# Three edits in a mixture-of-experts, scan and soft-expert kernel: gates spread by DMA, a first sequence started another way, eight logit tiles computed a stage earlier

## What is computed

```python
# 1. mixture of experts: a shared expert of 512 units, 8 routed experts of 128 units, top 2 of 8
s = sigmoid(x_flat @ router_w.T + t_bias)
combine = gates of the two largest s, zero for the other six        # [tokens, 8]
H = gelu(einsum('nd,ehd->enh', x_flat, rw1))
O = einsum('enh,edh->end', H, rw2)
cond = (shared_out + einsum('end,ne->nd', O, combine)) / 3
# 2. two selective scans (forward and on the flipped sequence), 512 channels x 16 states, 1024 steps
h = exp(delta * A) * h + (delta * u) * B ;  y_t = sum over states of h * C
# 3. gated mix of both directions, projection, residual, then a mask by a threshold per column
x1 = x + proj(g * y_f + (1 - g) * y_b) ;  xm = x1 where |x1| >= threshold
# 4. soft experts: 64 experts x 32 slots
logits = einsum('bmd,dnp->bmnp', xm, phi)
dispatch = softmax(logits, axis=0)            # over the two batches
combine = softmax(logits over all n*p)        # per token
out = x1 + combine-weighted sum of (slots @ W + b)
```

## Time and profile before

| what | value |
|---|---|
| median of 3 runs | 1508.34 us (1508.3 to 1510.53) |
| the profiled execution | 1510.97 us, of which 1509.2 us from the first to the last instruction |
| PE busy | 1202.4 us (80%) |
| DVE busy | 1144.5 us (76%) |
| POOL busy | 888.9 us (59%) |
| ACT busy | 776.6 us (51%) |
| mean granted PE clock | 0.889 of full |

### The profile page before, as it was taken

How to read it: one execution, slowest core, us unless ns; L and a number is a source line. 1 busy time by engine, 2 the same in 40 slices (tenths; PEclk the granted TensorE clock), 3 DMA queues, 4 the chain that set the end, 5 groups by cost and what they waited for, 6 DMA issues and landing times. The chain is left out here.

```text
span 1509.2 us, 14727 instructions
## 1 busy us (share of the span) xinstructions
PE 1202.4 (80%) x4972; PEld 670.6 (44%) x4972; DVE 1144.5 (76%) x1020; ACT 776.6 (51%) x1038; POOL 888.9 (59%) x395
## 2 busy tenths in 40 slices
PE   5899987698748897649887475473687999999998
PEld 4688842233203232113322121131246788787887
DVE  4433355999999999999999999999876544554544
ACT  5343456567546676545775555465255534343430
POOL 4420024999999999999999999999811000000000
PEclk9999999798868898769889788696798999999999
DMA  5133017322363342354223427312105030302012
GB/s 197 43 126 112 28 37 254 154 83 112 129 235 125 128 167 96 131 223 181 81 87 143 154 110 286 140 68 100 49 9 195 0 140 1 140 0 118 7 39 73
DMA packets 42544, 169.82 MB, mean 113 GB/s; under 512 B 5601, under 2 KB 10209, under 8 KB 30066
## 3 DMA queue, kind: packets, MB, share of 16 engines
q1 hardware_dynamic: 42482, 169.05, 30.2%
HBM read 136.53 MB, written 32.51 MB: 112 GB/s over the span
## 5 line engine op out<-in xcount | busy, mean ns | idle before, releaser
L1205 POOL TENSOR_TENSOR scan_dbu<-scan_rep,scan_bc 128x1024 f32<-128x1024 f32 x254 | 592.3, 2358 | 38.7 <-ACT scan_rep L1102 32.5
L1286 DVE TENSOR_TENSOR_SCAN scan_hs<-scan_hs,scan_dbu 128x1024 f32<-128x1024 f32 x189 | 432.2, 2287 | 15.7 <-ACT scan_hs L1131 14.1
L1131 ACT ACTIVATE scan_hs<-scan_rep,scan_neg_a 128x1024 f32<-128x1024 f32 x252 | 280.8, 1118 | 303.2 <-DVE scan_hc L1298 276.4
L1019 PE MATMUL scan_ysum<-scan_hc,scan_sel 128*32 128x512 f32 x1008 | 169.6, 804 | 208.5 <-DVE scan_hc L1298 193.1
L1298 DVE TENSOR_TENSOR scan_hc<-scan_hs,scan_bc 128x1024 f32<-128x1024 f32 x189 | 231.1, 1223 | 6.0
L1019 PEld LDWEIGHTS scan_ysum<-scan_hc,scan_sel 128*32 128x32 f32 x1008 | 35.3, 130 | 323.2 <-issue 269.5
L1211 POOL TENSOR_TENSOR scan_hc<-scan_hc,scan_bc 128x1024 f32<-128x1024 f32 x67 | 157.7, 2353 | 10.2 <-DVE scan_hc L1286 9.8
L1286 DVE TENSOR_TENSOR_SCAN scan_hc<-scan_hs,scan_dbu 128x1024 f32<-128x1024 f32 x67 | 152.7, 2279 | 2.0 <-POOL scan_dbu L1205 1.0
L899 PE MATMUL late_banks<-late_xin,scan_inwf 128*128 128x512 f32 x256 | 114.5, 601 | 0.0
L32 PE MATMUL ffn_sl<-ffn_tanh_s,xm_s 128*128 128x512 f32 x384 | 106.0, 411 | 2.3 <-DVE ffn_tanh_s L2031 2.3
L32 PE MATMUL moe_first<-moe_x_s,moe_w_s 128*128 128x512 f32 x384 | 98.3, 399 | 8.2 <-DVE moe_w_s L412 8.2
(11 more groups left out here) (234 smaller groups left out, 1732.0 us busy)
## 6 DMA issues: line engine op xcount, KB each, us to landing
scan_rep<-dd_rows SPq DMA_DIRECT2D x60, 1024.0 KB, 5.8
scan_bc<-bc_rows SPq DMA_DIRECT2D x32, 512.0 KB, 6.1
ffn_wt<-in_ew SPq DMA_DIRECT2D x16, 1024.0 KB, 7.3
dd_rows<-scan_dd SPq DMA_DIRECT2D x15, 1024.0 KB, 3.8
scan_inwf<-fold SPq DMA_DIRECT2D x12, 512.0 KB, 3.9
cond<-scan_bc SPq DMA_DIRECT2D x16, 256.0 KB, 3.1
y_all<-scan_yo SPq DMA_DIRECT2D x6, 512.0 KB, 3.1
scan_bc<-in_xT SPq DMA_DIRECT2D x4, 512.0 KB, 7.7
```

The source lines that it names most:

```text
L1019: mm = nc.tensor.matmul(ysum[i * D32:(i + 1) * D32, h, :], sel[:], hc[:, (s0 + i) % HCR, h * CT:(h + 1) * CT], start=False, stop=last, til ...
L1131: nc.scalar.activation(hs[:, s % HSR, :], rep[:, e % REPS, 0, :], ACT.Exp, scale=scale).then_inc(da_done, 1)
L1205: nc.gpsimd.tensor_tensor(dbu[:, s % DBR, :], rep[:, e % REPS, 1, :], bc[:, j, 0, :], ALU.mult).then_inc(dbu_done, 1)
L1286: nc.vector.tensor_tensor_scan(states, hs[:, s % HSR, :], dbu[:, s % DBR, :], 0.0, ALU.mult, ALU.add).then_inc(scan_done, 1)
```

## The change

Three edits that share a tile called `wide` (16 KB a partition). In the expert stage it holds the raw weights, in the scan stage the convolution's output of odd sequences (`uc[1]`), and from the mixing stage on the logits of one batch, and then the output sums.

1. Expert gates. In chunks 1 to 3 the expert units have no `factor`: the turned gates are copied to SBUF, stored to `gate_rows` in HBM, and SP loads each row to 128 partitions (`load_gates`, 8 DMAs of 256 KB a chunk). DVE's product reads this tile.
2. First sequence. The exponential of `neg_a` comes later on ACT. A memset goes from DVE to POOL. The first step's Relu on ACT and addition on DVE become two DVE operations that read PE's banks. PE writes the spread step straight into the decay slots (`spread_step`), the order of the spread is written out (`FIRST_SPREADS`), and DVE takes the first spread product from PSUM. Periods 0 and 1 have 3 pool units (0, 6, 11) where they had 4.
3. Last stage. PE makes the 8 logit tiles of batch 0, chunk 0, in the mixing stage ahead of every second one of the first 16 turns, and ACT copies them out. Chunk 0 of the last stage makes only batch 1's. The maximum over both is then two operations. Batch 1's `x1` rows are copied to tiles of their own (the old `gate` tile), with no wait for stores. The zeroing of the output sums goes behind chunk 0's exponentials.

```diff
+        def spread_gate(g):
+            return g >= UNITS and g % UNITS >= SU
...
+            def load_gates(c):
+                sp.wait_ge(hid_done, UNITS * c if c > 1 else 1)
+                for e in range(EXPERTS):
+                    sp.dma_start(wide_gate[:, e, :], gate_rows[c * E32 + e].partition_broadcast(P)).then_inc(gate_in[e // SU], 16)
...
+            sp.wait_ge(comb_ready, 2)
+            sp.dma_start(gate_rows, logit_sb[:]).then_inc(gate_in[0], 16)
+            sp.wait_ge(gate_in[0], 16)
+            sp.wait_ge(logits_done, 1)
+            load_gates(1)
             for c in range(NC):
                 b, h = divmod(c, CB)
+                if 0 < c < NC - 1:
+                    load_gates(c + 1)
...
             for g in range(SU + 3, NC * UNITS):
                 value(g)
-                factor(g)
+                if not spread_gate(g):
+                    factor(g)
                 project(g - 2)
...
+                if spread_gate(g):
+                    dve.wait_ge(gate_in[u // SU - 1], 16 * (SU * c + int(u < 2 * SU)))
+                    other = wide_gate[:, u - SU, :]
+                else:
+                    dve.wait_ge(factor_done, FACTORS[g])
+                    other = first[:, g % 3, 1, :]
                 dve.wait_ge(act_done, g + 1)
-                nc.vector.tensor_tensor(first[:, g % 3, 1, :], act_h[:, g % 2, :], first[:, g % 3, 1, :], ALU.mult
-                                        ).then_inc(hid_done, 1)
+                nc.vector.tensor_tensor(first[:, g % 3, 1, :], act_h[:, g % 2, :], other, ALU.mult).then_inc(hid_done, 1)
...
             nc.vector.tensor_copy(gates_s[:, 0, :], turned).then_inc(gates_ready, 1)
+            nc.vector.tensor_copy(logit_sb[:], turned).then_inc(comb_ready, 1)
...
-POOL_UNITS, LATE_POOL_UNITS = (0, 3, 7, 10, 13), (0, 4, 8, 12)
+FIRST_POOL_UNITS, POOL_UNITS, LATE_POOL_UNITS = (0, 6, 11), (0, 3, 7, 10, 13), (0, 4, 8, 12)
...
+FIRST_SPREADS = ((0, 0), (1, 0), (0, 1), (1, 1), (1, 2), (0, 2), (1, 3), (0, 3))
...
+            def spread_step(i):
+                if i >= HSR:
+                    wait_states(pe, i - HSR)
+                wait_delta(pe, 0)
+                for h in range(HALVES):
+                    mm = nc.tensor.matmul(hs[:, i % HSR, h * CT:(h + 1) * CT], spread[:, i * P:(i + 1) * P],
+                                          dd[:, 0, h * CT:(h + 1) * CT], start=True, stop=True)
+                mm.then_inc(spread_done, 1)
...
             def replica(i):
                 for h in range(HALVES):
-                    x, free = ready(act, "r", i, 1, h)
+                    x, free = ready(act, "r", i, h)
+                    if i == 0:
+                        act.wait_ge(dbu_done, 1)
...
-            nc.scalar.activation(neg_a[:], neg_a[:], ACT.Exp).then_inc(neg_done, 1)
             nc.scalar.preload_act_table_set("silu_and_others")
...
+            nc.scalar.activation(neg_a[:], neg_a[:], ACT.Exp).then_inc(neg_done, 1)
             act.wait_ge(neg_done, 2)
+            for kind, i in FIRST_SPREADS:
+                (decay, replica)[kind](i)
...
-            step_add(nc.vector, dve, 0)
+            dve.wait_ge(soft, HALVES + 2)
+            for h in range(HALVES):
+                x, free = ready(dve, "t", 0, 0, h)
+                own = dd[:, 0, h * CT:(h + 1) * CT]
+                nc.vector.scalar_tensor_tensor(own, x, 0.0, own, ALU.max, ALU.add).then_inc(free, 1)
             step_du(nc.vector, dve, 0)
...
+            def logits(m):
+                if m == 0:
+                    pe.wait_ge(kept["phi_split"], 1)
+                    pe.wait_ge(xt_low, KC)
+                    pe.wait_ge(gate_done, KC)
+                wait(pe, logits_read, m - 1)
+                for k in range(KC):
+                    mm = split_products(nc, pg[:, m % 2, :], [x[:, k, 0, m * P:(m + 1) * P] for x in xt_s],
+                                        [w[:, k, :] for w in kept["phi_s"]], k == 0, k == KC - 1)
+                mm.then_inc(logits_mm, 1)
...
-            for key in TURNS:
+            for g, key in enumerate(TURNS):
+                if g < 2 * MT and g % 2 == 0:
+                    logits(g // 2)
                 turn(*key)
...
-                        act.wait_ge(x1_stored[j % 2], 16 * TG // 2)
-                    nc.scalar.activation(turn_sb[j], tr[:, g % 2, :], ACT.Copy).then_inc(turn_read[g % 2], 1)
+                        act.wait_ge(y_done, KC * CB)
+                    nc.scalar.activation(turn_sb[b][j], tr[:, g % 2, :], ACT.Copy).then_inc(turn_read[g % 2], 1)
...
-                for b in range(BATCH):
+                for b in range(int(first), BATCH):
                     for k in range(KC):
                         mm = split_products(nc, lg[:, b, :], [x[:, k, b, m * P:(m + 1) * P] for x in xt_s],
...
-            nc.gpsimd.memset(acc[:], 0.0).then_inc(init_done, 1)
+            pool.wait_ge(exp_done, BATCH * MT)
+            pool.wait_ge(diff_done, MT)
+            nc.gpsimd.memset(acc, 0.0).then_inc(init_done, 1)
```

237 lines of the change are left out of this document (136 added, 101 removed).

## The result

The changed kernel takes 1500.31 us (median of 8 runs, 1495.5 to 1504.0), the kernel before beside it 1509.6 (8 runs, 1508.3 to 1513.5): ratio 0.9939, 95% interval 0.9924 to 0.9954, 9.3 us or 0.6% faster. Forecast were 1490.0 and a range up to 1498.5: the sign is right and half of the gain is missing. Profiled execution: 1501.33 us, span 1499.5 (before 1510.97 and 1509.2).

The account below looks back on a forecast made before the run. PE was taken to bound the expert and last stages, DVE to set the scan stage's pace beside a full POOL. Expert -8.4, scan front -4.0, mixing +1.5, last -7.4 sum to -18.3: median 1490.0 us, range 1484.5 to 1498.5.

Parts of the forecast that it names:

- term of +1.5 for the held product: Expert stage, chunk 1: DVE's product, both inputs in SBUF, held by POOL's four folding operations; +1.5 us (0 to +6).
- Rival (B): Expert stage: POOL holds DVE's product at each of four folding operations, margin under 0.53; +5 us, 1495, chance 0.10.
- term of +0.65: Expert stage: the new copy of the gates on DVE stands between two operations PE waits for; +0.65 us.
- step (a) to (c): Scan front: earlier first copy -0.7, Relus off ACT -0.5, shorter spread -2.3; first scan 3.5 us earlier.
- step (c): Scan front, spread written into decay slots: product with u to first scan takes 3.9 us, not 6.1; -2.3.
- what I had named as an end and not taken: Scan front: PE at half clock for the first spread records as before, about +1.5 us; left out of the sum.
- (d): Scan periods 0 and 1, 3 pool units: DVE's extra product of 1.2 us each is hidden; uncovered, +1.2 each.
- from then on DVE sets the pace, and a start that is earlier by some time ends earlier by the same: Scan stage: POOL holds DVE up just once, for 0.25 us, so the front's gain of 4.0 us lasts.
- rival (C): Scan stage: PE's sum for unit 11 comes 1.1 us later, DVE waits; +3.5 us, 1493.5, chance 0.11.
- +1.5 and -7.4: Mixing stage 1.5 us longer for the logits moved into it; last stage 7.4 us shorter without them.
- (A): Mixing stage: PE's clock falls between the turns; +11 us, 18 at worst, 1501, chance 0.12.
- (E): Mixing-stage logits displace nothing, first chunk held elsewhere: last stage gains 2 us, not 7.4; 1495.5, chance 0.09.

Follow-up runs that it names:

- filler of two: Changed kernel with pool units 0, 4, 8, 12 in the first two periods, plus two useless PE products ahead of the first skip product: 1489.75 us, 0.9842.
- new front with the old units: Changed kernel, but POOL weighs units 0, 4, 8, 12 in the first two periods: 1494.12, 1492.46 and 1494.95 us in three groups.
- filler of six: Changed kernel plus six useless PE products ahead of the first skip product, pool units unchanged: 1498.1 us, ratio 0.9904.
- old front: Changed kernel with its second edit undone (scan front and pool units as in the kernel before): 1496.28 us, 0.9897; one later run 1491.48.

## Why the prediction was wrong, point by point

**Expert stage: the gates' worth right, the two small terms not.** Between the marks the edit brings 11.0. The forecast had 10.6 (its 0.45 us a unit would give 10.4). The term of +1.5 for the held product was too dear: the four products during the folding grew by 0.45 to 0.56 us each, not by up to 1.8, the margin of 0.53 took nearly all of it, and PE lost 0.2 us. Rival (B) is out by the same rows. In two other profiles two of the four were held for 0.74 to 0.93, and the marks lie 0.3 to 0.4 further apart. The copy of the gates has a second price that the term of +0.65 lacks. It lengthened PE's idle time ahead of the gate products by 0.46, and behind it they took 2.73 us instead of 1.62, and the clock was 0.50 from 48 to 52 us. Timeline of PE, changed kernel (before: the earlier trace rows):
```profile
47.21 2.73 PE L284 MATMUL moe_first<-moe_gates_s,moe_ident_s 128*128 128x512 f32 x6 [2.05 <-issue]
50.56 2.90 PE L32 MATMUL moe_second<-moe_hid_s,moe_w_s 128*128 128x512 f32 x6 [0.62 <-DVE moe_hid_s L451]
```
From the first gate product to the mark it takes 16.2 us in all three profiles without the edit; with it, 16.2 in three, 16.7 to 16.8 in four and 18.3 in eight, the changed kernel's two among them. So the copy costs 0.5 to 2.6 us. That the longer idle time brings the half clock is argued from these counts; no run separates the two. Over 15 profiles with the edit the scan stage starts at 188.4 to 193.2 (median 190.4), over three without it at 198.8 to 201.1 (median 198.9): -8.5. That is the forecast's -8.4, with a larger gain and a dearer copy than it had. The -10.85 of the profiled pair is larger since PE's gate products began 2.2 us later in that profile of before than in its second.

**Front of the scan, step (a) to (c): the mechanism right, the size not.** Forecast -3.5, seen -0.9. Where the convolution's first products had full clock, the first scan came at 36.8 (four profiles; 37.5 in a fifth), that is -2.75; in the changed kernel's two profiles they had half. Windows of the changed kernel:
```profile
192.00:194.00 2.00, 2.00 (x4) 0.94 (x3) 0.00 (x0) 0.04 (x1) 0.00 (x0) 0.50 1.04 178
```
and of the kernel with units 0, 4, 8, second profile:
```profile
192.00:194.00 2.00, 2.00 (x6) 0.93 (x5) 0.00 (x0) 1.11 (x3) 0.00 (x0) 1.00 1.08 182
```
0.50 is 1.2 GHz, the lower of the clock's two levels. ACT's first copy stood 3.7 and 2.2 us after the stage's start. The rest is what I had named as an end and not taken: half the clock at the skip product and the first spread step (2.7 and 2.9 instead of 1.9), about 1 us by the filler of two. "The skip product is put in between" did not keep the clock, since 2.39 us of idle time lie ahead of it. From the end of the product with u to the first scan, for which step (c) had 3.9 us, it took 4.0 with the filler of two and 5.0 without (second profile of the new front with the old units). (d) held in period 0 for the units chosen: the scan of unit 16 starts at 95.4 in the changed kernel and in the one with 0, 4, 8, 12 whose first scan is as late.

**The step that failed: "from then on DVE sets the pace, and a start that is earlier by some time ends earlier by the same", and with it the weight given to rival (C).** I had seen in the earlier trace rows that POOL is full, and in the earlier trace rows that it held DVE once for 0.25 us, and took that small wait for a large margin. It was none. The two lists went side by side, and the edit gave POOL unit 11, whose product ends 17 operations of 2.3 us after POOL's second operation began (237.82 to 277.16). Rival (C) has this mechanism word for word, "PE's sum of a pool unit that stands last of its four (unit 11)", but "comes 1.1 us later", for which it gives no working. It came 4.0 us after DVE could have been through (277.31 against 273.3, by the 44.3 us that lie between first scan and third sum with units 0, 4, 8), because of the product's place in POOL's list. It is not DVE's head start that widens the gap: POOL's second operation began 8.87 us after the first scan, and 9.25 before the edit, so both lists moved together. 8.87 and the 17 operations make 48.2 us from the first scan to POOL's product, against the 44.3 that DVE needs, before the edit as well (83.9 - 39.6). And PE, idle for 4.87 us, then had half its clock, which added 1.7 at the sum and 1.0 at the projection. So (C) was mis-sized: I had +3.5 for it, at a chance of 0.11; in the trace it is +4.65 against the forecast, from first scan to first gated output. I had also looked at DVE's waits alone. What decides is ACT's list: a convolution output stands in it ahead of a decay, and joins PE's lateness to DVE.

**Later periods: forecast 0, seen +4.2, not settled.** No edit touches them. The waits that make it up stand where PE has half its clock. Timeline of PE in period 14, changed kernel:
```profile
987.11 3.64 PE L1065 MATMUL scan_ysum<-scan_hc,scan_sel 128*32 128x512 f32 x16 [3.97 <-POOL scan_hc L1262]
990.68 4.78 PE L995 MATMUL late_banks<-scan_dd,scan_ident 128*128 128x512 f32 x8
```
and the kernel before:
```profile
993.30 1.92 PE L1019 MATMUL scan_ysum<-scan_hc,scan_sel 128*32 128x512 f32 x16 [2.28 <-POOL scan_hc L1211]
995.15 3.70 PE L949 MATMUL late_banks<-scan_dd,scan_ident 128*128 128x512 f32 x8
```
The same two steps take 8.4 and 5.6 us, and ACT and DVE wait for them (2.64 us at 1005.51): that period has 55.8 us after and 53.0 before. This part is not unit 11's: the period has 55.7 or 55.8 in six profiles of kernels without it too, and one of these kernels (0, 4, 8) had 55.8 once and 53.0 once. Over all 18 profiles the stretch from first to last gated output is anywhere from 779.2 to 788.7 us. All four profiles of a scan stage that is exactly the changed kernel's (two of that kernel, and those without its first or its third edit) have 787.1 to 787.3, the kernel before 783.05 and 784.4: this speaks for order. Three others moved by 3.6 us (twice) and 5.6 us between executions: this speaks for chance. So does the filler of six, which leaves unit 11 and its wait of 3.86 us in place and has 783.5. Whether unit 11 costs any of these 4 us stays open. That the kernels without it are, by their ratios, 6 to 10 us below the changed one, where its own wait is 4, leaves room for it; that the filler of six is 5 below with unit 11 speaks against.

**Mixing stage and last stage: right in the profiled pair, in part by luck.** +1.4 and -7.65 for +1.5 and -7.4; first tile -1.9 as forecast, tile period 5.44 for 5.48, and 1.00 of the clock between the turns, so (A) and (E) are out. That +1.5 was -2.7 and +4.1 I had not told apart, and against the second profile of before it is -0.15. The last stage's gain is not the same in every execution either: in ten of the fifteen profiles with the moved logits the eighth tanh comes 43.6 us after the stage's start, in five at 45.4 to 45.8, since PE keeps half its clock for longer and the third tile comes 7.2 to 7.6 us after the second. A window and two tanh of ACT in the second profile of units 0, 4, 8 (its first profile had 5.44 between the two):
```profile
1142.00:1150.00 8.00, 5.95 (x14) 3.98 (x14) 5.32 (x12) 3.21 (x8) 0.00 (x0) 0.50 0.97 368
...
1150.23 0.63 ACT L2034 ACTIVATE ffn_tanh<-ffn_tanh 128x512 f32<-128x512 f32 x1 [2.33 <-DVE ffn_tanh L2118]
...
1157.80 0.63 ACT L2034 ACTIVATE ffn_tanh<-ffn_tanh 128x512 f32<-128x512 f32 x1 [2.34 <-DVE ffn_tanh L2118]
```
"PE runs thinner at the start, where it is at half clock" had 0.2 us for this.

**Sum.** In the profiled pair the scan stage is 11.4 us off (7.45 instead of -4.0), and the expert stage gave 2.45 back. Against the medians: forecast 18.3, got 9.3. With the units put back (and nothing else) the same edits bring 18.5, 19.5 and 20.8 against the medians of before beside them (1510.94, 1514.45, 1514.9, which stood 1 to 5 us above that of the first series); their own medians are 1492.5, 1495.0 and 1494.1. So the forecast's gain is nearly that of a kernel with POOL's old units. That the figures meet is partly luck, since the gates, their copy, the front and the two terms of the mixing stage each came out at another size. The low end of the range has no working: the bounds of the first two terms give 1487.6, and no term leads to 1484.5.

## What to carry to other kernels

A short wait for a full second engine says nothing about its margin for other items. Ask of a unit that is given to the full engine where it stands in that list, not only how many there are: count the operations from the list's start to the item, times what one takes, and compare with the time at which its reader has all else. Here that is 48.2 against 44.3 us after the first scan. Follow a late item through all lists in which its consumer queues: here POOL's product reached DVE through PE and ACT. Before a gap on PE is filled to hold the clock, count its records in the trace: two products brought the first scan 1.0 us forward, six put it back by up to 1.0.

## What the runs showed of the hardware that was not expected

DVE and POOL, both with two inputs in SBUF, slowed one another down: DVE's product 0.70 to 1.26 us, POOL's operation 2.40 to 2.86. The size of the hold follows a simple count. In all 15 profiles with the edit, for each of the four products, the hold is what was left of POOL's operation when the product began, less 0.13 to 0.16 us. The rest was 0.49 to 1.07 us and the hold 0.34 to 0.93. So the product waits until POOL's operation is through, and POOL's next one then waits for the product: the two lists fall into step, and each costs the other some 0.5 us. The Trainium skill (SBUF — State Buffer, Who interferes with whom) speaks of an exclusive lock; the trace agrees. What the forecast had too dear is how much of POOL's operation would be left when a product begins.

The granted clock is a state that a kernel does not repeat from run to run: in two executions of one kernel the same 16 records (the third sum, old front) take 1.92 and 2.86 us, the first six gate records 1.63 us in some and 2.6 to 2.9 in others, and one and the same kernel showed 783.1 and 788.7 us for 15 periods. A single profile of this kernel can't carry a difference of under some 5 us; a wait that stands at the same place in all five profiles with units 0, 6, 11 (3.86 to 4.25 us) can.
